# A graph layer on one core: sums joined on VectorE from PSUM, h and its residual in other buffers and pieces

## What is computed

```python
h = jnp.maximum(_layernorm(x, axis=-1), 0.0)          # x: 6250 nodes x 96, f32
m = h[src] + edge_attr                                # 206250 edges x 96, sorted by dst
aggr = jax.ops.segment_sum(m, dst, num_segments=6250)
hidden = jax.nn.relu(aggr @ W1 + b1)                  # 96 -> 192
mlp_out = hidden @ W2 + b2                            # 192 -> 96
out = (1.0 + eps[0]) * h + mlp_out
x = x + out
```

## Time and profile before

| | us |
|---|---|
| three runs | 562.74, 560.37, 561.38 |
| median | 561.38 |
| the profiled execution | 559.85 |
| its span in the trace | 558.0 |
| PE busy | 499.2 |
| DVE busy | 504.6 |
| ACT busy | 375.2 |
| POOL busy | 353.9 |

### The profile page before, as it was taken

How to read it: one execution, slowest core, us unless ns; L and a number is a source line. 1 busy time by engine, 2 the same in 40 slices (tenths; PEclk the granted TensorE clock), 3 DMA queues, 4 the chain that set the end, 5 groups by cost and what they waited for, 6 DMA issues and landing times.

```text
span 558.0 us, 23440 instructions
## 1 busy us (share of the span) xinstructions
PE 499.2 (89%) x9695; PEld 474.5 (85%) x9695; DVE 504.6 (90%) x676; ACT 375.2 (67%) x613; POOL 353.9 (63%) x200
## 2 busy tenths in 40 slices
PE   0406798999999999999999999999999999999995
PEld 0305788999999999999999999998998999999994
DVE  7989997999999999899998998998998989999840
ACT  0486556677777757776875677677776776775771
POOL 1400048888888888888888887687686478870000
PEclk9999879999999999999999999999999999999998
DMA  6789849999879888999888889988878687985000
GB/s 196 244 283 286 245 122 318 277 307 271 234 196 234 230 210 207 290 262 236 230 232 215 210 217 266 285 215 224 227 206 223 158 241 179 236 226 172 6 11 18
DMA packets 99109, 120.57 MB, mean 216 GB/s; under 512 B 71160, under 2 KB 72792, under 8 KB 98870
## 3 DMA queue, kind: packets, MB, share of 16 engines
q1 hardware_dynamic: 74854, 108.13, 63.3%
q0 software_dynamic: 24144, 10.89, 15.5%
HBM read 112.50 MB, written 6.48 MB: 213 GB/s over the span
## 4 chain that ended last, share of the span: by engine, by line
PE 76%; SPq 7%; ACT 4%; issue 4%; DVE 3%; DMA 3%; POOL 2%; ACTq 0%; DVEq 0%; POOLq 0%
PE agg_ps L973 27%; PE oct_ps L961 21%; PE agg_ps L967 14%; PE key_ps L986 5%; PE mlp_ps L991 4%; SPq L340 3%; ACT adj L810 3%; POOL gathered_edges L477 2%; PE key_ps L978 2%; PE key_ps L979 2%; SPq L339 1%; SPq L341 1%; DMA win<-packed_keys,row_i 1%; ACT hid L826 1%; DVE lo_hot L547 1%
## 5 line engine op out<-in xcount | busy, mean ns | idle before, releaser
L810 ACT ACTIVATE adj<-oct_ps 128x784 f16<-128x784 f32 x360 | 300.6, 867 | 146.9 <-PE oct_ps L961 141.5
L477 POOL DMA_INDIRECT gathered_edges<-h_rows,gather_src x160 | 317.8, 1986 | 97.6 <-DMA gathered_edges<-in_edge_attr 49.1
L973 PE MATMUL agg_ps<-hl,adj 128*128 128x192 f16 x2205 | 227.7, 247 | 0.9 <-issue 0.8
L547 DVE TENSOR_TENSOR lo_hot<-iota_z,key 128x2048 f16<-128x2048 f16 x180 | 219.4, 1219 | 0.0
L961 PE MATMUL oct_ps<-z,lo_hot 128*128 128x98 f16 x2880 | 191.5, 209 | 25.3 <-DVE lo_hot L547 21.0
L547 DVE TENSOR_TENSOR z<-z_marks,key 128x1568 f16<-128x1568 f16 x180 | 174.6, 970 | 22.1 <-PE oct_ps L961 21.7
L961 PEld LDWEIGHTS oct_ps<-z,lo_hot 128*128 128x128 f16 x2880 | 162.5, 99 | 33.5 <-issue 13.9
L973 PEld LDWEIGHTS agg_ps<-hl,adj 128*128 128x128 f16 x2205 | 177.1, 98 | 1.9 <-issue 1.4
L967 PE MATMUL agg_ps<-edges,hot 128*32 128x96 f32 x3440 | 81.1, 250 | 0.0
L967 PEld LDWEIGHTS agg_ps<-edges,hot 128*32 128x32 f32 x3440 | 71.8, 111 | 6.4 <-issue 0.3
L674 DVE TENSOR_TENSOR hot<-iota_w,rel 128x1280 f32<-128x1280 f32 x49 | 73.1, 1492 | 1.7
(11 more groups left out here) (126 smaller groups left out, 204.2 us busy)
## 6 DMA issues: line engine op xcount, KB each, us to landing
edges<-in_edge_attr SPq DMA_DIRECT2D x172, 480.0 KB
gathered_edges<-in_edge_attr SPq DMA_DIRECT2D x24, 480.0 KB
dst<-in_dst SPq DMA_DIRECT2D x180, 5.0 KB
gathered_edges<-h_rows,gather_src POOLq DMA_INDIRECT x160
out<-ob SPq DMA_DIRECT2D x45, 48.0 KB
packed_keys<-adj SPq DMA_DIRECT2D x1, 1632.0 KB, 6.3
h_rows<-edges SPq DMA_DIRECT2D x1, 1200.0 KB, 9.2
h_rows<-edges SPq DMA_DIRECT2D x1, 1152.0 KB, 9.2
```

Source lines behind the costliest of these rows:

```text
L477: nc.gpsimd.indirect_dma_start(out=gathered[k][:, g, t, :], out_offset=None, in_=h_dram, in_offset=bass.IndirectOffsetOnAxis(ap=gather_src ...
L547: return nc.vector.tensor_tensor(out.rearrange("p t (w two) -> p t w two", two=2), marks[0:out.shape[0], 0:width].rearrange("p (o w two) - ...
L810: return nc.scalar.activation(adj[k][:, :, 2 * OCT * o:2 * OCT * (o + 1)].rearrange("p h (t q) -> p t h q", q=2), oct_ps[:, o % 2, :].rear ...
L973: last = nc.tensor.matmul(agg_ps[buf][:, 0:2 * C], adj[buf][:, h, :], hl[:, h, :], start=False, stop=(h == NT - 1), skip_group_check=True)
```

## The change

Seven edits, most of which move work:

- **Sums.** ACT's copy of 192 columns (`take_sums`) goes. DVE adds the two halves while it reads them from PSUM, with one `tensor_reduce` into `agg`, now 96 columns wide (`join`), and PE turns that by one transposition (`turn_sums`). In block b DVE does `next_join(b - 2)` between its chunks 1 and 2, where it waits until PE has finished the slots of block b-2.
- **h.** It is written by ACT alone, 49 rows, with the statistics in thirds of 16, 16 and 17 rows (`THIRDS`), and stands in the gathered blocks' two buffers. The edges of blocks 1 and 2 go straight to their own buffers.
- **Residual.** Nine pieces (`RES`): rows 40 to 48 at the end of DVE's block 2, then five rows at the end of each of the blocks 3 to 10.
- **SP.** `load_gathered(0)`, which stood ahead of `load(4)`, now follows `load(5)`, which waits for the edges of block 2; `load_gathered(1)` follows `load(14)`.
- **POOL.** One window more is fetched before the gathers, and then three in 25 gathers (before: one in 7).
- **ATTACHED.** The second and third gathered block are summed in blocks 22 and 32, not 24 and 34.
- **Order at the start.** Some small reads of PSUM (`span`, `ends`) come later on DVE, and PE's first octet waits for them (`spread_read` 2).

```diff
-ATTACHED = (14, 24, 34, 42)
+ATTACHED = (14, 22, 32, 42)
-FETCH_EVERY = 7
-FETCH_FIRST = 5
+FETCH_EVERY = 25
+FETCH_PER = 3
-SQRT_AFTER = 18
-KEYS_AFTER = 20
+KEYS_AFTER = 24
+RES_FIRST = 40
+RES_ROWS = 5
...
-        h_sb = edge_home[:, 1:3, :, :, :].rearrange("p k g t c -> p (k g t c)")[:, 0:NT * C].rearrange("p (t c) -> p t c", c=C)
+        h_sb = gather_home[:, :, :, :, :].rearrange("p k g t c -> p (k g t c)")[:, 0:NT * C].rearrange("p (t c) -> p t c", c=C)
...
+        THIRDS = [slice(0, 16), slice(16, 32), slice(32, NT)]
+        RES = [(RES_FIRST, NT)] + [(t, t + RES_ROWS) for t in range(0, RES_FIRST, RES_ROWS)]
...
         def edge_rows(b):
-            return gathered[b % 2] if b in (1, 2) else edges[b % TURN]
+            return edges[b % TURN]
...
             for b in range(TURN, NM):
                 sp.wait_ge(edges_done, b - TURN + 1)
-                if b == TURN + 1:
-                    load_gathered(0)
-                    sp.wait_ge(res_ready, 2)
-                    sp.wait_ge(h_stored, 32)
                 load(b)
                 if b == TURN + 2:
+                    sp.wait_ge(h_stored, 32)
+                    sp.wait_ge(res_ready, 1)
+                    load_gathered(0)
+                if b == TURN + 2 + len(RES):
+                    sp.wait_ge(res_ready, len(RES))
                     load_gathered(1)
...
-            fetched = WINS
+            fetched = WINS + 1
+            fetch(WINS)
             pool.wait_ge(h_stored, 32)
...
-                        if (j * GROUPS + g) * GT + t >= (fetched - WINS) * FETCH_EVERY + FETCH_FIRST and fetched < MPAIRS:
+                        if ((j * GROUPS + g) * GT + t) * FETCH_PER >= (fetched - WINS - 1) * FETCH_EVERY and fetched < MPAIRS:
...
-            for t in range(HALF, NT):
-                last = nc.vector.tensor_scalar(h_sb[:, t, :], x_sb[:, t, :], rstd[:, t:t + 1], shift[:, t:t + 1], ALU.mult, ALU.add)
-            last.then_inc(scaled_ready, 1)
...
+            def join(k):
+                return nc.vector.tensor_reduce(agg[:, :], agg_ps[k][:, 0:2 * C].rearrange("p (two c) -> p c two", two=2), AX_X, ALU.add)
+
+            def next_join(n):
+                v.wait_ge(agg_done, n + 1)
+                if n >= 1:
+                    v.wait_ge(aggT_done, n)
+                join(n % 2).then_inc(sums_ready, 1)
...
+                if b >= 2:
+                    next_join(b - 2)
                 if b == 1:
                     low_part(1)
                 for c in range(2, CHUNKS):
                     chunk(b, c)
-                if b in (1, 2):
-                    residual(b - 1)
+                if 2 <= b < 2 + len(RES):
+                    residual(b - 2)
...
-            for t in range(HALF):
-                if t == KEYS_AFTER:
-                    next_keys(0)
-                if t == SQRT_AFTER:
-                    deviation(1)
+            for t in range(NT):
+                for k in range(1, 3):
+                    if t == THIRDS[k].start:
+                        deviation(k)
+                for k in range(3):
+                    if t == THIRDS[k].start:
+                        act.wait_ge(norm_ready, k + 1)
+                last = nc.scalar.activation(h_sb[:, t, :], x_sb[:, t, :], ACT.Relu, bias=shift[:, t:t + 1], scale=rstd[:, t:t + 1])
...
-            act.wait_ge(scaled_ready, 1)
-            nc.scalar.activation(h_sb[:, ROWS[1], :], h_sb[:, ROWS[1], :], ACT.Relu).then_inc(h_ready, 1)
...
-                if b >= 2:
-                    next_sums(b - 2)
...
-            def turn_both():
-                nc.tensor.matmul(key_ps[0:C, TURN_AT:TURN_AT + P], agg[:, 0:C], ident[:, :], start=True, stop=False)
-                return nc.tensor.matmul(key_ps[0:C, TURN_AT:TURN_AT + P], agg[:, C:2 * C], ident[:, :], start=False, stop=True)
+            def turn_sums():
+                return nc.tensor.transpose(key_ps[0:C, TURN_AT:TURN_AT + P], agg[:, :], ident[:, :])
```

87 lines of the change are left out of this document (45 added, 42 removed).

## The result

| | kernel before | changed kernel |
|---|---|---|
| runs of that comparison | 8 | 8 |
| median, us | 559.31 | 564.31 |
| lowest and highest | 557.81 to 562.74 | 562.51 to 568.00 |
| a second comparison, median | 558.96 | 564.73 |
| span of the profiled execution | 558.0 | 566.2 (561.2 in the second) |

What follows compares the result with a forecast made beforehand. PE was taken as the bound, DVE close behind. 296.4 + 264.0 - 7.9 + 2.6 + 0.5 = 555.6, 2.4 us under the span of 558.0, so 561.38 - 2.4 = 559.0 us; range 553.5 to 563.5.

Steps and rivals of the forecast that it cites:

- the arrival at 296.4: In block 22, PE can sum gathered block 1 at 296.4, having asked at 288.3, so it stands 8 us.
- The rest of the sum: After the arrival: 264.0 us as before, less 7.9 for 24 transpositions, plus 2.6 cold clock and 0.5 late DVE.
- first gather: POOL's gathers begin at 92.2, 14.8 us later than before, behind SP's load that waits for block 2's edges.
- to the eightieth: POOL's first eighty gathers: 200.9 us as before, less 1.6 for one window fewer, so the eightieth comes at 291.5.
- from there to PE's sum: Landing of the eightieth gather before PE's sum in block 22: 4.9 us, the median of windows' 4.2 to 6.2.
- the gathers get slower: Rival, chance 0.14: POOL's issues stretch beside a DVE without pause; 0.03 us on each of 80 uses up the gain.
- the rule that it cited: DVE and GpSimd share ports under an exclusive lock; by the rule the join and hot values don't touch the gathers.
- The transposition: On PE, one transposition replaces products with the identity: 0.33 us less in each of 45 blocks, 14.9 us.
- The join: DVE's reduction from PSUM takes 0.27 us a block, bounds 0.17 and 0.54, from a copy of 200 columns.
- DVE as the bound of blocks 4 to 13: DVE takes 10.87 us a block with a residual piece, 10.27 after; block 14's edges at 201.5.
- DVE's block 0: At the start DVE waits for ACT's rows of h, so its block 0 begins at 39.3 to 39.5, before at 39.55.
- The cold array behind the stall: After idling 8 us in block 22 PE starts at a cold clock, which costs 2.6 us.

Runs made afterwards that it cites:

- noz: Changed kernel without DVE's one-hot values z from block 4 on (wrong sums, only its times count): 546.95 us in one run.
- nosums_b: Changed kernel with the sums as before (ACT's copy of 192 columns, two products with the identity): 563.67 us, 1.0062 of the kernel before.
- after_b: The changed kernel as it is, run once more in a second job: 564.73 us, 1.0091 of the kernel before.
- start1: Changed kernel, residual pieces one block earlier, gathered block 0 loaded ahead of block 4's load: 548.37 us, 0.9800 of the kernel before; again 562.86 us, 0.9741.

## Why the prediction was wrong

Its mechanism was the right one, PE waiting in block 22 for gathered block 1, and the step that failed is **the arrival at 296.4**: it was 306.1 in one profile and 303.8 in the other. The rest of the sum, from there to the end, was worked out as 259.2 us (264.0 - 7.9 + 2.6 + 0.5) and measured 260.1 and 257.4. With the arrival put right by 7.4 to 9.7 us the forecast turns from a gain of 2.4 into a loss of 5 to 7.

| term of the arrival | worked out | first profile | second |
|---|---|---|---|
| first gather | 92.2 | 97.69 | 97.05 |
| to the eightieth | 199.3 | 201.94 | 203.04 |
| from there to PE's sum | 4.9 | 6.50 | 3.68 |
| sum | 296.4 | 306.13 | 303.77 |

**The first gather, 5.5 and 4.9 us.** The steps up to SP held: the edges of block 2 end at 73.0, SP issues at 74.08 (73.8). In the first profile two of its issues then take 1.33 and 1.87 us in place of 0.33:

```profile
81.13 1.33 SPq L351 DMA_DIRECT2D gathered_edges<-in_edge_attr  x1
...
86.25 1.87 SPq L351 DMA_DIRECT2D gathered_edges<-in_edge_attr  x1
...
89.86 0.33 SPq L351 DMA_DIRECT2D gathered_edges<-in_edge_attr  x1
```

With 0.3 at the start they make the last piece 2.86 us late. POOL's first instruction follows 5.59 us after it (5.19 worked out). In the second profile no issue of this load is that long, and POOL's first instruction is at 92.71, 0.5 us from the 92.2 worked out for the first gather. Yet the first gather is as late in it, because that first instruction is no gather but a window:

```profile
92.71 4.04 POOL L451 DMA_INDIRECT win<-packed_keys,row_i  x1 [62.81 <-PE key_ps L968]
```

With the new pacing a window is due at gather 0. It keeps POOL 2.24 us in the first profile (95.45 to 97.69) and 4.34 in the second (92.71 to 97.05). The text took one window fewer between the first gather and the eightieth, and none ahead of the first. The condition in the diff gives two fewer (nine, and eleven before) and one ahead. So 1.6 us for this window were in the sum, but in the next term. The place could have been read off; the long issues could have been a bound, since the earlier trace rows are all of 0.33 but for the neighbours at 1.20 and 1.63 that were left out of the group.

**The pace, 4.2 and 5.3 us.** With two windows fewer the text's own figures give 197.7 us from the first gather to the eightieth (200.9 - 3.2), and not 199.3; measured were 201.94 and 203.04. A gather's record has a mean of 2.00 us before and of 2.05 and 2.03 after, which is 2.6 to 3.5 us for eighty; the rest lies with the windows. Put together, the first profile's 9.7 us are 3.3 for SP and the landing of its load, 0.6 for the window beyond the 1.6 counted, 4.2 for the pace and 1.6 for the last landing; the second's 7.4 are 0.5, 2.7, 5.3 and -1.2. **The pace is the largest part in both.**

The text took 2.3 us a gather from before and let windows alone change it. `noz` shows that the pace depends on DVE. Before, DVE still had its wait of 2.69 us in block 4, and a gather that overlaps the wait's end (95.86) is in line with that:

```profile
94.89 1.55 POOL L477 DMA_INDIRECT gathered_edges<-h_rows,gather_src  x1 [0.30 <-issue]
96.74 1.71 POOL L477 DMA_INDIRECT gathered_edges<-h_rows,gather_src  x1 [0.30 <-issue]
```

The change filled this gap. But that doesn't give the size: over the eighty gathers DVE stood idle for 9.6 us before and for 7.2 and 8.5 after, while in `noz` 51 us more of idle DVE were worth 15.7. By that rate, an estimate, 1.1 to 2.4 us less of idle DVE cost 0.3 to 0.7 us. The changed kernel without the join has the pace of before (197.6 against 197.7), which points at the join; above it says how far this is shown. What slowed the pace stays open beyond that. So the rival "the gathers get slower" (0.14) was right in kind, and its price was about right: 0.03 to 0.04 us on each of 80 in the records, and with the windows more than the gain of 2.4. The text gave that rival a price and let it keep its chance against the rule that it cited. The Trainium skill (SBUF — State Buffer, Who interferes with whom) also says that a DVE instruction with two SBUF inputs contends with a GpSimd instruction that reads SBUF. The operations left out in `noz` have two SBUF inputs, and a gather reads its indices from SBUF; the 15.7 us between 187.3 and 203.0 agree with that sentence, and not with the use that the prediction made of the section. Which port it is, no run here shows.

**Steps that were right.** The transposition: one record, 0.20 us to the edges. The join: 0.27 us, with 0.35 in the record, as assumed from the copy of 200 columns. DVE as the bound of blocks 4 to 13: block 14's edges at 201.49, forecast 201.5. DVE's blocks 2 and 3 and the warm clock of block 2. DVE's block 0 came at 38.0 and not at 39.3 to 39.5, with the wait for ACT that was named (4.20 us); PE's octets of block 0 then waited 4.08 us for ACT, so nothing followed from it. The cold array behind the stall took less than the 2.6 us forecast: from the start of the gathered sum to block 23's edges are 12.65 and 11.71 us in the two profiles, and the same stretch at block 32, without a stall, takes 10.80 and 10.75, so 1.9 and 1.0 us. Late blocks without a stall or a gathered block take 10.03 and 10.28 us in turn (10.17 forecast).

**A step missed without effect.** In block 14 PE already waited 2.28 us for the gathers, and in the first profile then summed at a granted clock of 0.53:

```profile
205.62 3.36 PE L979 MATMUL agg_ps<-gathered_edges,hot 128*32 128x96 f32 x80 [2.28 <-DMA gathered_edges<-h_rows,gather_src]
```

In the second the wait was longer, 2.51 us, and the clock stayed at 1.00:

```profile
205.22 1.86 PE L979 MATMUL agg_ps<-gathered_edges,hot 128*32 128x96 f32 x80 [2.51 <-DMA gathered_edges<-h_rows,gather_src]
```

Block 22's edges came at 291.79 (289.27 in the second profile) and not at 286.5, for that wait and for smaller gaps. It cost nothing in the end, as PE asked at 293.6 for what came at 306.1.

**Why a change meant to save PE work cost time.** In the changed kernel the gathers set the time up to block 22, so nothing that PE or DVE save before it counts: `nosums_b` is as fast as `after_b`. Behind it the 24 transpositions do count, 6.7 us between these two profiles, of which the 4.3 us by which the gathers came later with the join take the larger part back. What is left is that the gathers start late, and `start1` takes it away: -16 us against the changed kernel. Its start is 17.5 us earlier; its eighty gathers took 3.1 us less as well.

## What to carry to other kernels

When a change delays a long serial stream (here 160 gathers of 2.5 us each with windows between, some 400 of 560 us) and lets its consumer ask earlier, add up the arrival as carefully as the saving: every instruction on the queue ahead of the first item, and the pace beside the neighbours as they will be. Here 37 us lay between the eightieth gather's issue and PE's use of it, some 5 of them for the landing; a start 20 us later and a consumer 22 us earlier used up more than that. And measure a saving on the bounding engine again after that wait is gone: the same sums were worth nothing in one order and 6 to 8 us in another.

## What the runs showed of the hardware

- An indirect DMA of POOL keeps it 1.54 us beside an idle DVE and 1.9 us in the median, up to 4.2 (`after_b`), beside a busy one. Leaving out four `tensor_tensor` operations of 0.97 us a block took 15.7 us off eighty gathers and the nine windows between them. Three gathers of 4.17 us in the changed kernel (at 115.57, 137.31, 159.07) stand at the same place of DVE's sequence each time, 21.75 us apart, the length of two DVE blocks. The same window took 1.93 us in one profile of the changed kernel and 4.04 in the other.
- SP's issue of a 480 KB load is 0.33 us in most rows and 1.0 to 1.9 in 15 of 196; in one profile two of them made a load of four pieces end 2.5 us later.
- After 12.49 us without work PE's next 3.5 us ran at a granted clock of 0.50, after 1.40 us, in block 2, there was no loss. In between the profiles differ: after 2.28 us of waiting the next 3.4 us ran at 0.53 in one, and after 2.51 us there was no loss in the other (nor after 2.39 us before). So the length of the gap alone doesn't tell.
- The kernel before took 559 to 561 us in three jobs and 577 to 580 in two, and the changed kernels stood better against it there: the one with blocks 14, 24, 34, 42 at 0.9943 and 0.9741, `start1` at 0.9800 and 0.9741.
